# One transformer-block kernel, one core: another order of all five engines' calls inside its step loop

## The reference, cut to what matters

```python
# layer 0, 8 heads of 40
hs      = mha(x @ Wq, enc @ Wk, enc @ Wv)          # enc: 124 context rows ("first" attention)
ca_q1   = einsum('btc,th->bch', ca, Wq_ca)[:, indices]   # ca: the 4 last context rows (tokens)
ca_hs1  = mha(ca_q1, x, x)                          # "ca" attention
ca_hs2  = mha(ca_hs1 @ Wq, ca @ Wk_ca, ca @ Wv_ca)  # 4 keys
x       = (hs + ca_hs2) @ Wout + b_out + x
# layer 1, 20 heads of 16
x = attn(ln1(x), ln1(x), q1, k1, v1) @ o1_w + o1_b + x      # "self"
x = attn(ln2(x), context, q2, k2, v2) @ o2_w + o2_b + x     # "cross"
a, g = split(ln3(x) @ ff_w1 + ff_b1)
out = (a * gelu(g)) @ ff_w2 + ff_b2 + x
```

## Time and profile before

| | us |
|---|---|
| median of 3 runs | 4264.14 |
| lowest and highest run | 4252.62, 4288.17 |
| the profiled execution's own time | 4277.24 |
| its span | 4275.4 |

### The profile page before, as it was taken

One profiled execution on the slowest core, in us unless ns is written; L12 is line 12 of the kernel. 1 busy time (PEld: TensorE's weight loads), 2 busy tenths in 40 slices (PEclk: granted clock), 3 DMA queues, 4 the chain that ended last, 5 costly groups with the idle time before them and its releaser, 6 DMA issues.

```text
span 4275.4 us, 114798 instructions
## 1 busy us (share of the span) xinstructions
PE 3770.2 (88%) x39220; PEld 3046.2 (71%) x39220; DVE 2761.4 (65%) x6482; ACT 2324.6 (54%) x3900; POOL 1974.6 (46%) x2297
## 2 busy tenths in 40 slices
PE   4888888988888998888989888989888898988889
PEld 4777677777777777766777777777777677777777
DVE  7666666666666666666665666666666666666665
ACT  1555555655555565555556455556555555655554
POOL 0445444444554444554444354444445444444543
PEclk9999999999999898999989898989999999999999
DMA  4332221333222133322223322213232221333221
GB/s 132 57 57 51 49 50 41 58 58 59 54 52 48 39 60 56 59 55 46 51 41 60 58 52 49 50 38 61 56 60 54 49 50 41 58 58 59 54 51 29
DMA packets 393942, 230.78 MB, mean 54 GB/s; under 512 B 24806, under 2 KB 393054, under 8 KB 393182
## 3 DMA queue, kind: packets, MB, share of 16 engines
q1 hardware_dynamic: 393566, 224.70, 26.7%
HBM read 148.59 MB, written 76.02 MB: 53 GB/s over the span
## 4 chain that ended last, share of the span: by engine, by line
issue 54%; POOL 29%; PE 11%; DVE 3%; ACT 1%; POOLq 1%; DMA 0%; SPq 0%; DVEq 0%
POOL PT L501 16%; PE bank L1377 11%; POOL cQ L508 3%; POOL XB L478 2%; POOL rstd L550 2%; POOL cK L508 2%; POOL XA L478 1%; POOL rstd L549 1%; POOL X L478 1%; ACT PT L725 1%; POOL ca L541 1%; POOL ca L539 0%; POOL ca L537 0%; POOLq L500 0%; ACT P L724 0%
## 5 line engine op out<-in xcount | busy, mean ns | idle before, releaser
L501 POOL TENSOR_TENSOR PT<-P,PT 128x512 f16<-128x512 f32 (+1 forms) x924 | 1066.8, 1158 | 1252.2 <-ACT PT L725 1252.2
L976 DVE TENSOR_REDUCE mx<-bank 128x4 f32<-128x512 f32 (+1 forms) x924 | 577.9, 679 | 230.2 <-PE bank L1377 228.8
L1377 PE MATMUL bank<-hT,w_ff_w 128*128 128x256 f16 x5440 | 634.0, 273 | 1.1 <-issue 0.9
L1377 PEld LDWEIGHTS bank<-hT,w_ff_w 128*128 128x128 f16 x5440 | 522.5, 98 | 69.2 <-issue 7.7
L1377 PE MATMUL bank<-mxs,pick 84*128 84x128 f16 (+1 forms) x3696 | 548.5, 229 | 0.0
L1377 PE MATMUL bank<-w_ff,F 128*128 128x320 f32 x1360 | 401.4, 438 | 1.3 <-DVE F L1052 1.3
L1377 PE MATMUL bank<-Qs,Ks 96*128 96x128 f16 x2640 | 394.0, 229 | 8.2 <-DVE mxs L985 6.1
L1377 PEld LDWEIGHTS bank<-mxs,pick 84*128 84x128 f16 (+1 forms) x3696 | 390.6, 108 | 10.6
L1377 PEld LDWEIGHTS bank<-V,PT 128*128 128x128 f16 (+1 forms) x9504 | 313.6, 96 | 72.2 <-POOL PT L501 42.6
L1377 PE MATMUL bank<-Ks,Qs 96*128 96x128 f16 x2640 | 242.6, 241 | 133.3 <-DMA Qs<-scratch_q 133.2
L1377 PE MATMUL bank<-V,PT 128*128 128x17 f16 (+1 forms) x9504 | 343.2, 173 | 5.3 <-POOL PT L501 5.3
(11 more groups left out here) (283 smaller groups left out, 8057.4 us busy)
## 6 DMA issues: line engine op xcount, KB each, us to landing
Ks<-scratch_k SPq DMA_DIRECT2D x198, 160.0 KB, 4.5
Qs<-scratch_q SPq DMA_DIRECT2D x198, 160.0 KB, 6.3
scratch_k<-cK SPq DMA_DIRECT2D x134, 128.0 KB, 1.8
scratch_q<-cQ SPq DMA_DIRECT2D x134, 128.0 KB, 2.0
Q0s<-scratch_q SPq DMA_DIRECT2D x99, 160.0 KB
K0s<-scratch_k SPq DMA_DIRECT2D x99, 160.0 KB
cT<-in_cT SPq DMA_DIRECT2D x136, 96.0 KB, 1.9
xin<-in_x SPq DMA_DIRECT2D x34, 320.0 KB, 3.0
```

The lines of the kernel that those rows point to most:

```text
L501: nc.gpsimd.tensor_tensor(PT[0:keys, n % PT_SLOTS, 1, :], P[0:keys, n % P_SLOTS, :], PT[0:keys, n % PT_SLOTS, 0, :], ALU.subtract).then_in ...
L976: nc.vector.tensor_reduce(mx[:, g % 2, 4 * u:4 * u + 4], bank[:, :].rearrange("p (h s) -> p h s", h=4)[:, :, 0:keys], axis=AX.X, op=ALU.ma ...
L1377: return nc.tensor.matmul(o, lhsT, rhs, start=start, stop=stop)
```

## The change

No instruction's work changes, with one exception: the first attention's scores are taken over 128 keys, where 124 were taken (the maxima still read 124). All else is order. On PE, `Q0T0` and `Q0T1` lead the step, then the normalised rows are turned and `S0`, `S1` follow; `M4` moves from before the self scores into the feed-forward part; `kca` from the top of the step to behind `K0T1` ("token keys under the stack loads"); `T3` and one more `attend` stand ahead of `S4`; `mT` and `mB` move into the feed-forward part; `K2T1` and `K2T2` go ahead; `outT1_1` stands behind `ff3`. On POOL, `x_values` and `token_queries` move ahead of unit 14. On ACT, `exp4` goes behind the last gelu. On SP, the reads of `Q0s` go behind those of `Ks` and `Qs`. The ACT and POOL loops get the hint at the back edge that PE and DVE had.

```diff
@@ BODY
-    XT0_0 XT0_1 kca Q0T0 Q0T1 Q0T2 K1T0 K1T1 K1T2 Q1T0 Q1T1 Q1T2 S0 S1 S2 K0T0 S3 vca M4 mx0 V1_0
...
+    Q0T0 Q0T1 XT0_0 XT0_1 S0 S1 Q0T2 K1T0 K1T1 K1T2 Q1T0 Q1T1 Q1T2 S2 mx0 S3 T0 T1 vca mx1 V0_0 T2
+    K0T0 V1_0 T3 K0T1 kca K0T2 V1_1 S4 S5 S6 S7 S8 V0_1 mx2 T4 S9 S10 S11 S12 T5 S13 caT0 T6 mx3 T7
...
+    XT1_1 s4 Q2T0 Q2T1 Q2T2 ff6 mT ff7 mB ff8 ff9 S14 S15 S16 S17 y1 S18 S19 mx4 K2T0 T14 S20 T15
...
@@ SP, one_pass
-                stack_first_queries(i)
                 put_split(i, "K1T", 2, cK, s_k1, self_put)
...
                 stack_self(i)
-                load_next(i)
-                stack_cross_keys(i)
+                stack_first_queries(i)
...
@@ POOL
-            with pool.Fori(0, STEPS + 1) as i:
+            with nc.Fori(0, STEPS + 1, engines=[pool.engine], hint_back_edge=True) as i:
                 links[0] = 0
-                last_bias(i)
-                first_bias(i, 0)
...
                 second_bias(i, 1)
+                x_values(i, 0, OA)
+                x_values(i, 1, OA)
+                token_queries(i)
                 low_probabilities(i, 14)
...
-                token_queries(i)
                 assert links[0] == POOL_LINKS
@@ ACT
-                exp4(i)
                 gelu(i, L, 6)
                 gelu(i, L, 7)
                 gelu(i, L, 8)
                 gelu(i, L, 9)
+                exp4(i)
                 load_exp_table()
@@ DVE
                 ff(i, L, 6)
-                softmax4(i)
+                diagonal(i, L)
                 ff(i, L, 7)
+                factors(i, L)
                 ff(i, L, 8)
...
+                softmax4(i)
+                low_chunk(i, "K2T", 2, cK, CH1[2], FK2)
                 maxima(i, 26)
@@ PE, scores
-                    q, k = operands(att, b, 4 * u + h)
-                    last = mm(bank[:, h * S:h * S + keys], q, k)
+                    q, k = operands(att, b, 4 * u + h, S)
+                    last = mm(bank[:, h * S:(h + 1) * S], q, k)
```

More of the change, by code:

```diff
@@ L109 @@
 BODY = jobs_of("""
-    XT0_0 XT0_1 kca Q0T0 Q0T1 Q0T2 K1T0 K1T1 K1T2 Q1T0 Q1T1 Q1T2 S0 S1 S2 K0T0 S3 vca M4 mx0 V1_0
[L111 to L116, removed]
+    Q0T0 Q0T1 XT0_0 XT0_1 S0 S1 Q0T2 K1T0 K1T1 K1T2 Q1T0 Q1T1 Q1T2 S2 mx0 S3 T0 T1 vca mx1 V0_0 T2
+    K0T0 V1_0 T3 K0T1 kca K0T2 V1_1 S4 S5 S6 S7 S8 V0_1 mx2 T4 S9 S10 S11 S12 T5 S13 caT0 T6 mx3 T7
+    T8 T9 T10 T11 T12 T13 caT1 ff0 outT1_0 ff1 ff2 ff3 outT1_1 outM1_0 ff4 outM1_1 ff5 XT1_0 M4
+    XT1_1 s4 Q2T0 Q2T1 Q2T2 ff6 mT ff7 mB ff8 ff9 S14 S15 S16 S17 y1 S18 S19 mx4 K2T0 T14 S20 T15
+    S21 S22 S23 K2T1 T16 mx5 S24 T17 S25 K2T2 T18 T19 T20 S26 T21 mx6 T22 T23 S27 y0 outT2_0 mx7 T24
+    T25 p4T T26 outM2_0 T27 hs0 outT2_1 V2_0 outT0_0 hs1 outM2_1 V2_1 outT0_1 outM0_0 outM0_1 XT2_0
+    XT2_1 G
 """)
@@ L748, in _ @@
             load_exp_table()
-            with act.Fori(0, STEPS + 1) as i:
+            with nc.Fori(0, STEPS + 1, engines=[act.engine], hint_back_edge=True) as i:
                 L = LOOP_JOBS
                 order.restart()
+                high_chunk(i, "Q0T", 0, cQ, CH0[0], FQ0)
+                high_chunk(i, "Q0T", 1, cQ, CH0[1], FQ0)
                 high_blocks(i, "XT0_0", hTn, 0)
                 high_blocks(i, "XT0_1", hTn, 1)
-                high_chunk(i, "Q0T", 0, cQ, CH0[0], FQ0)
-                high_chunk(i, "Q0T", 1, cQ, CH0[1], FQ0)
                 high_chunk(i, "Q0T", 2, cQ, CH0[2], FQ0)
@@ L1242, in _ @@
                 order.restart()
+                low_chunk(i, "Q0T", 0, cQ, CH0[0], FQ0)
+                low_chunk(i, "Q0T", 1, cQ, CH0[1], FQ0)
                 low_blocks(i, "XT0_0", hTn, 0)
                 low_blocks(i, "XT0_1", hTn, 1)
-                token_keys(i)
-                low_chunk(i, "Q0T", 0, cQ, CH0[0], FQ0)
-                repeat_tokens(i)
-                low_chunk(i, "Q0T", 1, cQ, CH0[1], FQ0)
+                maxima(i, 0)
+                maxima(i, 1)
                 low_chunk(i, "Q0T", 2, cQ, CH0[2], FQ0)
@@ L1485, in scores4, with operands @@
                 last.then_inc(j_full, 1)
-            def operands(att, b, head):
+            def operands(att, b, head, keys):
                 s = slice(b * S, (b + 1) * S)
@@ L1492, in operands @@
                 if att == FIRST:
-                    return Q0s[:, head, s], K0s[:, head, b * S:b * S + KEYS0]
+                    return Q0s[:, head, s], K0s[:, head, b * S:b * S + keys]
                 return Qs[:, head, s], Ks[:, head, s]
@@ L1498, in scores @@
                 att, b, u = ALL_UNITS[n]
-                keys = KEYS[att]
                 if (b, u) == (0, 0):
@@ L1528, in exponents @@
                 for h in range(4):
-                    q, k = operands(att, b, 4 * u + h)
+                    q, k = operands(att, b, 4 * u + h, keys)
                     o = bank[0:keys, h * S:(h + 1) * S]
@@ L1765, in _ @@
                 ff(i, L, 6)
+                extremes_turned(i, L)
                 ff(i, L, 7)
+                extremes_everywhere(i, L)
                 ff(i, L, 8)
```

248 lines of the change are left out of this document (123 added, 125 removed).

## The result

Four runs of the changed kernel on the chip that also ran the kernel before took 4132.51 us (median; 4125.89 to 4142.58), against 4262.36. The ratio is 0.969, with a 95% interval of 0.966 to 0.973: 3.1% faster, where 7.4% was forecast (3950 us, range 3840 to 4110). The direction is right, and the time is outside the range. The profiled execution has a span of 4124.0 us.

The account below looks back on a forecast made before the run. PE was taken as the bound, with its waits and low clock to be cut. Savings of 2.7 + 2.6 + 0.7 + 2.5 + 1.0 = 9.5 us a step, 314 us over 33 passes, gave 3950 us, range 3840 to 4110.

Parts of the forecast that it names:

- The step's end: Last attend to PE's restart: without ca_heads line 966 is short, 1.7 us of waits stay, 2.7 us a step saved.
- The clock at the step's start: Q0T products: without the 3.8 us wait ahead they run at full clock, 2.6 us a step saved.
- Behind the last Q1T product: Up to S4: two new waits, 2.1 and 1.1 us, replace one of 4 us; S4 starts 0.7 us earlier.
- S4 to ff0: From S4 to the feed-forward products: 13.6 us if the clock doesn't fall ahead, 2.5 us a step saved.
- nothing like a low clock follows from them alone: Claim that PE's small waits, 0.6 to 1.0 us each, do not by themselves bring a low clock.
- Those that the clock survives: Waits of 1.0 us at most, set against those of 3.2 and 3.8 us after which the clock fell.
- The feed-forward part: ff3 ahead of outT1_1 hides its wait for OB: 1.0 us a step saved.
- costs about that much: s4 as only cover of the last block before Q2T loses about what M4's 1.7 us at the second turn hides.
- ACT: exp4 behind the gelus saves ACT two table loads, 2.6 us a step, priced at nothing because PE doesn't wait for ACT.
- the clock still falls once: Rival: clock falls at the waits behind Q1T as often as now, 6 us a step lost, 4066 us; chance 0.2.
- The small rest: ACT and POOL loop hints bring nothing; 128 keys in place of 124 cost under 0.03 us a step.
- Unit 14: POOL's token work ahead of unit 14 fits its idle time: the unit is not late, with 1 us to spare.

Follow-up runs that it names:

- e3: The changed kernel with POOL's x_values back behind units 23 and 24 and token_queries behind unit 27; 1.059 of the kernel before.
- e18: The changed kernel with M4 and outM1_1 moved ahead of ff4 and ff5; 4089 us, 0.960 of the kernel before.
- e12: The kernel before with exp4 alone moved behind the last gelu and its softmax behind the maxima of S19; 1.001 of the kernel before.
- e9: The changed kernel with exp4 alone put back between the gelus; 0.995 of the kernel before.
- e15: e9 with 2 useless float32 matmuls (1.8 us) ahead of the wait of T0; 4104 us, 0.960 of the kernel before.
- e10: The changed kernel without the ACT and POOL loop hints, reads of Q0s back, first scores over 124 keys; 0.966 of the kernel before.
- e5: The changed kernel with 2 useless float32 matmuls (1.8 us) ahead of the wait of T0; 4081 us, 0.957 of the kernel before.
- e13: e18 with vca and V0_0 also moved ahead of T0 and K0T0 ahead of T2, no filler; 4002 us, 0.937 of the kernel before.
- e14: e13 with DVE's copy of the token columns early and V0_1 ahead of S4; 3985 us, 0.933 of the kernel before.
- e17: e14 with 3 useless float32 matmuls (1.6 us) in PE's wait ahead of mx2; 3923 us, 0.921 of the kernel before.
- e16: The changed kernel with 2 useless float32 matmuls (1.8 us) ahead of mB, exp4 left in place; 4247 us, 0.994 of the kernel before.

## Why the prediction was right or wrong

- **The step's end** (2.7 us): right. Line 966 went to 0.23 us and the wait for `G` to nothing; the turn of `OA` kept 21.5 / 33 = 0.65 us and `outM0_1` got 0.72: 1.4 us of waits for the 1.7 taken. That POOL's large instruction held line 966 is what the Trainium skill (SBUF — State Buffer, § Who interferes with whom) states; its absence in the trace after agrees, and so does e3, where the two don't meet either. What the term is worth in time was not tried by itself.
- **The clock at the step's start** (2.6 us): right, it is full in every step from `Q0T` to `K1T`.
- **Behind the last Q1T product** (0.7 us) and **S4 to ff0** (2.5 us): the waits were right to 0.3 us each (1.86 for 2.1 at `T0`; about 1.0 for 1.1 at unit 0; `T4` 0.8 for 1.0; 15.5 us to `S4` at full clock for 15.2). The step that failed is the sentence "nothing like a low clock follows from them alone", and with it the "if it doesn't fall" of the 13.6 us. Low clock gave 1.5 us back ahead of `S4` and 1.1 behind it. The trace of the kernel before had spoken against that sentence, in the very step of the earlier trace rows. There the wait for `G` begins at 1359.57 - 3.85 = 1355.72 us. Ahead of it PE had waited 0.63 us for `OA` and run the 12 matmuls of 8 columns of `kca`. The clock is full up to 1355.70 and low right behind it, so it fell as the long wait began, and not behind it:

```profile
1352.00:1355.70 3.70, 3.07 (x23) 2.39 (x21) 3.55 (x12) 1.68 (x4) 3.11 (x6) 1.00 0.00 0
1355.80:1359.50 3.70, 0.00 (x0) 0.00 (x0) 3.63 (x3) 0.00 (x0) 3.70 (x2) 0.50 0.00 0
```

Of the 32 falls at a step's end of that kernel 11 begin within 0.9 us of the start of the wait for `G`. "Those that the clock survives", 1.0 us at most, was therefore no bound: the prediction looked at which long wait stood near the low clock, and not at when the clock fell.

- **The feed-forward part** (1.0 us): the wait of `outT1_1` did go, but "costs about that much" for `M4` next to `s4` was wrong: 0.85 us of a new wait and 5.1 us of low clock a step. e18 took both away, with the short wait and the small matmuls moved together, so which of the two brings the clock down is open.
- **ACT** (nothing): the 2.6 us of ACT's two table loads were rightly called hidden for the old order (e12). In the new one they would not be: with `exp4` back, PE waits 1.47 us a step for `diag` (e9, e15), so the condition "where PE never waits for it" does not hold there. (The 1.28 us of the earlier trace rows are the row of the load alone; whether a switch costs ACT more than that row was not looked at.) And `exp4`'s move carries 2.6 of the 3.1 points, since without it every step falls behind `T0`. In this sense the prediction's rival "the clock still falls once" was the right one (4066 us): it named the place and the waits, and was given 0.2. It took one fall, and there are three places, `T0` and `mx2` in half the steps and `s4` in all, so its 4066 is 67 us short too.
- **The small rest** (nothing): right (e10).
- **Unit 14**: right. POOL is done with the token work 1.0 us before ACT is with the unit (POOL's timeline, one step of the kernel after):

```profile
1766.84 3.60 POOL L542 TENSOR_TENSOR ca_heads<-ca,mask_ca 96x2048 f16<-96x2048 f16 x1
1771.47 1.16 POOL L501 TENSOR_TENSOR PT<-P,PT 128x512 f16<-128x512 f32 x1 [1.04 <-ACT PT L725]
```

In sum: 9.5 us a step forecast, 4.6 in the profiled execution ((4275.4 - 4124.0) / 33). The missing 4.9 us are low clock for the most part: 13.2 us a step at half speed cost up to 6.6, e18's steps without a fall put the changed kernel's at some 116 us (an estimate, above) for the 120.4 measured, and e5, e13, e14 and e17, which took 3.6, 5.4, 6.4 and 13.2 us of it away, gained 1.2, 3.4, 3.8 and 5.0% over the changed kernel (e13, e14 and e17 with some 1 to 2 us of waits in it). What remains open is why a wait of 1.86 us with the same work ahead of it brings the clock down in one step and not in the next. That time added at one place decides it, and not what PE does in that time, is shown (e9, e16); the rule behind it was not tried by itself, nor was work added where no wait stands at another place.
